# Folding the stage between the layers into the second layer's pipeline

## What is computed

```python
x_prev = jnp.concatenate([jnp.zeros((B, 1, D)), x[:, :-1]], axis=1)
write_lines = exterior(x_prev @ w1w.T, x @ w2w.T)      # per head, 6 components, unit length
read_lines = exterior(x @ r1w.T, x @ r2w.T)
Jw = einsum('bthi,ij->bhtj', write_lines, _J6)
outer = Jw[..., :, None] * Jw[..., None, :]            # 6 x 6, symmetric
M_all = decayed cumulative sum of outer over t, shifted by one token
rd_M = einsum('bhti,bhtij->bhtj', rd, M_all)
score_M, score_M2 = sum(rd_M * rd), sum(rd_M * rd_M)
mem_score = (1 - alpha) * score_M + alpha * score_M2
gated = mean over heads of sigmoid(mem_score * mem_scale) * sigmoid(x @ memg_w.T + memg_b)
out = (seq_out + gated * (x @ memv_w.T + memv_b)) @ out_w.T + out_b
```

## Time and profile before

| | us |
|---|---|
| median of 3 runs | 2576.94 |
| the three | 2562.86, 2576.94, 2578.11 |
| profiled execution, device time | 2571.01 |
| its span | 2569.2 |
| mean granted TensorE clock | 0.888 of 2.4 GHz |
| TensorE, VectorE, ScalarE, GpSimd busy | 86%, 52%, 39%, 14% |

### The profile page before, as it was taken

One profiled execution on the slowest core, in us unless ns is written; L12 is line 12 of the kernel. 1 busy time (PEld: TensorE's weight loads), 2 busy tenths in 40 slices (PEclk: granted clock), 3 DMA queues, 4 the chain that ended last, 5 costly groups with the idle time before them and its releaser, 6 DMA issues. The chain is left out here.

```text
span 2569.2 us, 38948 instructions
## 1 busy us (share of the span) xinstructions
PE 2203.8 (86%) x13569; PEld 1547.9 (60%) x13637; DVE 1340.0 (52%) x3927; ACT 995.6 (39%) x3145; POOL 362.7 (14%) x639
## 2 busy tenths in 40 slices
PE   8588888889999987897727789899999999999887
PEld 4266665656777764676514456566666666766654
DVE  7245556464635454321149457565656565666441
ACT  3133535445454534352212245444434344444320
POOL 2044252332504142001000000000000000000000
PEclk9767989888899978997859699999999999999988
DMA  8000000001233111445550000000000000000000
GB/s 305 9 5 1 5 5 10 9 9 32 97 103 106 44 38 51 154 175 194 166 168 0 15 10 5 6 5 10 5 5 10 5 10 5 6 5 5 5 1 9
DMA packets 50763, 116.27 MB, mean 45 GB/s; under 512 B 8192, under 2 KB 30464, under 8 KB 46976
## 3 DMA queue, kind: packets, MB, share of 16 engines
q1 hardware_dynamic: 49024, 109.49, 12.6%
q0 software_dynamic: 1536, 4.20, 0.5%
HBM read 90.20 MB, written 23.46 MB: 44 GB/s over the span
## 5 line engine op out<-in xcount | busy, mean ns | idle before, releaser
L690 ACT ACTIVATE PRS<-PT 128x384 f32<-128x384 f32 (+1 forms) x512 | 266.1, 520 | 653.7 <-PE PT L621 653.5
L755 DVE TENSOR_REDUCE negmax<-SM 128x2 f32<-128x512 f32 x432 | 283.5, 685 | 194.3 <-PE SM L584 96.7
L621 PE MATMUL PT<-const_sb,PRS 128*128 128x128 f32 x1664 | 309.6, 304 | 51.7 <-ACT PRS L690 49.5
L705 ACT ACTIVATE PRS<-SM,negmax 128x128 f32<-128x128 f32 x608 | 248.1, 420 | 184.8 <-DVE negmax L755 184.8
L621 PEld LDWEIGHTS PT<-const_sb,PRS 128*128 128x128 f32 x1664 | 206.1, 153 | 147.6 <-issue 97.6
L2758 DVE TENSOR_SCALAR arena<-arena 128x256 bf16<-128x256 bf16 x1024 | 210.3, 279 | 9.9 <-PE SC L2776 9.0
L574 PE MATMUL SM<-haloU,QM 32*128 32x128 f32 (+1 forms) x1056 | 172.9, 376 | 7.1 <-ACT PRS L705 4.7
L574 PEld LDWEIGHTS SM<-haloU,QM 32*128 32x128 f32 x1056 | 131.2, 216 | 22.8 <-ACT PRS L705 8.6
L2776 PE MATMUL SC<-arena,identb 128*128 128x256 bf16 x1024 | 138.2, 278 | 2.4 <-DVE arena L2758 2.4
L636 PE MATMUL OA<-PRS,big 128*32 128x256 f32 (+1 forms) x1024 | 133.7, 387 | 3.0 <-ACT PRS L690 3.0
L574 PE MATMUL SC<-haloU,QM 32*128 32x128 f32 (+1 forms) x480 | 111.3, 388 | 28.3 <-ACT PRS L705 28.3
(11 more groups left out here) (565 smaller groups left out, 4072.3 us busy)
## 6 DMA issues: line engine op xcount, KB each, us to landing
...
arena<-lay SPq DMA_DIRECT2D x1, 7700.5 KB, 21.4
...
arena<-lay SPq DMA_DIRECT2D x1, 3862.0 KB, 20.6
...
```

What stands on the lines that cost most here:

```text
L621: ins = pe.transpose(bank[:, o:o + P], PR[n % 4][:, t, k * P:(k + 1) * P], ident)
L690: act.activation(dst, src, ACT.Copy).then_inc(S("probs_moved"), 1)
L705: ins = act.activation(dst, src, ACT.Exp, bias=negmax[:, h, r:r + 1], accum_out=rsum[:, t, h:h + 1])
L755: st.post(dve.tensor_reduce(negmax[:, ORDER[s], :], two(banks[s % NB]), AX.X, ALU.max, negate=True), S("max_ready"))
```

## The change

The stage between the layers and the `clear_block` behind it go. Two new threads of layer 1 do its work. `memory` (30 pieces) has the gate: VectorE's exteriors; squares on ScalarE instead of VectorE; per row i only the components j >= i of the symmetric matrix (21 scans instead of 36), from which two tiles of products are made (`ROW_A`: the row, `ROW_B`: its mirror in the columns), summed by TensorE in SC, PJ0 and PJ1. `fold` (31 pieces) has the same products, in another order, through the one bank "a". The loads of `feat`, `gate_d` and of the weights stand at the head of layer 1's SyncE program, the weights in three parts, in this order: the first 2560 columns (`lay1_a`), the last 2310 (`lay1_b`, biases and small tables), the 10531 between (`lay1_c`). The piece "turn x" of start(1) writes to a second tile (`XNs`), GpSimd clears `VS_count` once the gate is done, and the feed-forward part takes the products under exchanged names (`fW{1 - br}`, `fV{1 - br}`).

```diff
-        SMs = [SM[0], SM[1], SC]
-        with nc.Block() as block:
...
-                for i in range(6):
-                    fold_pe(pe, 0 if i == 0 else 16 + 3 * (i - 1), 16 + 3 * i)
-                    pe.wait_ge(S("row_ready"), i + 1)
...
-        clear_block()
-
...
+        def fold_pe(pe, ba):
+
+            for u, (pe_part, _) in enumerate(folds):
+                if u == 0:
+                    pe.wait_ge(S("lay1_a"), 16)
+                    pe.wait_ge(S("lay1_b"), 16)
+                if u == FOLDS_FIRST:
+                    pe.wait_ge(S("lay1_c"), 16)
+                ba.fill(pe_part(pe, ba.claim(pe)), "act")
+                yield
+
+        def fold_act(act, sa, ba):
+
+            for u, (_, act_part) in enumerate(folds):
+                bank = ba.take(act, "act")
+                ba.release(sa, act_part(act, bank), "act")
+                sa.settle()
+                yield
...
+        MEMORY_LOOP = [[(0, 6, (0, 3)), (0, 6, (3, 6)), "rows"], [(1, 5, (1, 3)), (1, 5, (3, 6)), "rows"], [(2, 4, (2, 6)), "rows"],
+                       [(3, 3, (3, 6)), "rows"], [(4, 2, (4, 6)), "rows"], [(5, 1, (5, 6)), "rows"]]
+        MEMORY = 10 + sum(len(part) for part in MEMORY_LOOP) + 6
...
+                    if part == "rows":
+                        if i:
+                            dve.wait_ge(S("row_summed"), i)
+                        st.post(dve.tensor_tensor(ROW_A[:, i:6, :], MM[:, i:6, 0:T], bc(RDP[:, i, :], 6 - i), ALU.mult), S("row_ready"))
+                        if i < 5:
+                            st.post(dve.tensor_tensor(ROW_B[:, i:5, :], MM[:, i + 1:6, 0:T], RDP[:, i + 1:6, :], ALU.mult), S("row_ready"))
...
+            act.wait_ge(S("feat_in"), 16 * (B + 1))
...
+            yield from idle(3)
+            pe.wait_ge(S("gated_ready"), 1)
...
-            chains(opened(0))
-            tally(0, (("hot", 0, HOT_FIRST + HOT_REST),))
-            chains((("middle", 0, JOIN),), opened(1))
-            for i in range(1, B):
+            chains((("memory", 0, 4),), (("start", 0, OPEN - 1), ("fold", 0, FOLDS_FIRST)))
+            tally(0, (("memory", 0, MEMORY - 10),), (("fold", 0, FOLDS - FOLDS_FIRST), ("start", 1, 1)))
+            chains((("memory", 0, 6), ("start", 0, 1)), (("start", 1, OPEN - 2),))
+            chains((("start", 1, 1), ("middle", 0, JOIN)), (("hot", 0, HOT_EARLY),))
+            tally(1, (("hot", 0, HOT - HOT_EARLY), ("ask", 0, TURN)))
+            count(0, (("middle", 1, JOIN),), opened(2), (("hot", 1, HOT),))
+            for i in range(2, B):
...
                 sp.dma_start(X1s[0][:], x4_d[1]).then_inc(S("x_in0"), 16)
+                for i in range(B):
+                    sp.dma_start(big[i * H:(i + 1) * H, 0:4096].rearrange("h (m n) -> h m n", m=4),
+                                 feat[i + 1].rearrange("m (h c) t -> h m (c t)", h=H)).then_inc(S("feat_in"), 16)
+                sp.dma_start(Z[:, 0, :], gate_d[1:B + 1].rearrange("b h t -> (b h) t")).then_inc(S("feat_in"), 16)
+                sp.dma_start(arena[:, 0:LAY1_A], lay1[:, 0:LAY1_A]).then_inc(S("lay1_a"), 16)
+                sp.dma_start(arena[:, LAY1_B:LAY1_N], lay1[:, LAY1_B:LAY1_N]).then_inc(S("lay1_b"), 16)
+                sp.dma_start(arena[:, LAY1_A:LAY1_B], lay1[:, LAY1_A:LAY1_B]).then_inc(S("lay1_c"), 16)
```

597 lines of the change are left out of this document (324 added, 273 removed).

## The result

| | before | after |
|---|---|---|
| median, us | 2577.5 (4 runs, 2562.9 to 2578.3) | 2617.3 (4 runs, 2608.0 to 2620.6) |
| ratio | | 1.0168, interval 1.0129 to 1.0206 |
| profiled execution, its span | 2571.0, 2569.2 | 2620.6, 2618.8 |
| mean granted TensorE clock | 0.888 | 0.880 |
| TensorE, VectorE, ScalarE busy, us | 2204, 1340, 996 | 2255, 1321, 1002 |

The changed kernel is 1.7% slower by the ratio, and 40 us by the two medians. I had said 2577, no change, in a range up to 2608. Runs in a slower state of the chip are left out of every ratio and median here: one of e8 (3639.1 us) and two of the kernel before (5008.1 and 2756.4 us). The two profiled executions are 49.6 us apart, 10 more than the medians; what follows accounts for the 49.6, and finds some 6 of them to belong to the one profiled execution and not to the change.

What follows compares the result with a forecast made beforehand. Took TensorE, nearly full, as the bound, with 82 of 311 us idle to win. Stages end at 1458 + 45 + 48 + 64 = 1615 against 1612, + 3 us: 2577 us, no change, range 2553 to 2608.

Steps and rivals of the forecast that it cites:

- no change: Whole kernel: the favoured outcome, 2577 us, its own range 2556 to 2600, chance 0.75.
- Loading: Start of layer 1: features land at 1319.5, first two weight parts at 1325.7, the third by about 1340.
- start(0) and four products: After the weights: 16.9 us for start(0)'s chain and 9.6 for four product steps at 1.2 GHz; tally(0) begins at 1352.2.
- tally(0): Attention with 27 product steps and five row sums woven in: 100 us plus 6 for the clock, ending at 1458.
- The rival of the swinging clock: tally(0): half of TensorE's busy time in slots 1 to 9 at 1.2 GHz, + 31, 2608 us; chance 0.12.
- Gate's end, start(1), middle(0): Between tally(0) and tally(1): gate's tail 13.4, value and memory pieces 15, middle(0) 16.5; together 45 us, where now 18.
- tally(1): Attention with 13 one-hot groups on TensorE, not 8, and late ask pieces: 39.8 + 5 x 1.05 + 3 = 48 us.
- count(0): 16 one-hot groups instead of 8: 56.4 + 7.6 = 64 us, VectorE busy 55 of these, no bound.
- a rival for tally(0) alone: tally(0): interlocks, a row's 3 us wait as in slot 4 in all ten slots, + 27, 2604 us; chance 0.04.
- The clock: TensorE's clock: + 6 us in tally(0), 0.5 until a slot's full stretch lifts it; 0 if high, + 19 if low.
- All behind that is the same list.: After count(0): same list of instructions; forecast called wrong if the stretch from 1612 on changes by over 5 us.

Runs made afterwards that it cites:

- e8: Changed kernel without weaving, products on two banks, the gate's last four pieces and start(0)'s last one beside tally(0): 2562.3 us, ratio 0.9938 to the kernel before.
- e4: Changed kernel without weaving: gate beside start(0) and all products first, through one bank, then tally(0) with one-hot groups: 2580.0 us, ratio 1.0018 to the kernel before.
- e5: Kernel before with all 16 one-hot groups of hot(1) in count(0), four buffers and TensorE using each two steps later: 2584.4 us, ratio 1.0037.
- e9: Changed kernel with four buffers for hot(1) and TensorE taking each group two steps later: 2599.7 us, ratio 1.0114 to the kernel before.
- e1: Kernel before with one added line: in each feed TensorE waits for VectorE's copy of XF: 2580.1 us, ratio 1.0020.
- e11: e8 with hot(0) moved into the time of the loads and the small weights loaded ahead of the features: 2553.0 us, ratio 0.9922 to the kernel before.
- e15: e11 with 14 filling matmuls ahead of the wait for the gate's first row: 2541.3 us, ratio 0.9895 to the kernel before.
- e6: Changed kernel with 26 of the gate's 30 pieces, its end among them, in tally(0): 2620.3 us, ratio 1.0188 to the kernel before.
- e10: Changed kernel with start(1)'s first three pieces ahead of the gate's last matmul on TensorE: 2609.8 us, ratio 1.0163 to the kernel before.
- e13: Changed kernel with 34 unused matmuls on TensorE ahead of its wait for the first weights: 2607.8 us, ratio 1.0143 to the kernel before.
- e7: e4 with its products alternating between two banks in place of one: 2566.7 us, ratio 0.9968 to the kernel before.
- e12: e11 with the features ahead of the weights in the queue, 12 pieces of hot(0) ahead of start(0): 2559.5 us, ratio 0.9936 to the kernel before.
- e2: Kernel before with all 16 one-hot groups of hot(1) in count(0) in place of 8, tally(1) keeping ask(0) alone: 2595.5 us, ratio 1.0082.

## Why the prediction was wrong, point by point

- **Loading.** Right. Features 1321.6 (1319.5 said), weights 1327.5 (1325.7). Timeline of ScalarE and VectorE, first work on each:

```profile
1321.57 0.20 ACT L2555 ACTIVATE small<-const_sb 128x1 f32<-128x1 f32 x1 [32.18 <-DMA Z<-gate_d]
...
1327.44 0.23 DVE L3125 TENSOR_TENSOR gate_s<-parq,arena 128x2 f32<-128x2 f32 x2 [28.19 <-DMA arena<-lay]
```

- **start(0) and four products.** 28.1 us for 26.5, clock 0.50 as said. First scores 1355.6 for 1352.2.
- **tally(0).** Right in the main: 110.4 us for 106, busy 81% for 80, VectorE 56% for 65. The product steps of a slot in TensorE's timeline:

```profile
1394.43 1.98 PE L2334 MATMUL PT<-AM,OUT 128*128 128x512 f32 x4 [0.69 <-ACT arena L2338]
1397.17 1.98 PE L2334 MATMUL PT<-AM,OUT 128*128 128x512 f32 x4 [0.75 <-ACT arena L2338]
```

and a stretch of such slots:

```profile
1373.00:1404.00 31.00, 23.72 (x109) 11.18 (x108) 20.06 (x27) 14.11 (x40) 0.00 (x0) 0.99 0.00 1
```

The steps are 2.74 us apart, 2.7 said. The wait for VectorE's first row was 2.8 us, 3.0 said.
- **The rival of the swinging clock** did not happen in tally(0): 0.99 in this stretch with TensorE busy 77% in cycles through one bank, and 1.00 in e4's. The one fall in these slots lasted 3 us, from 1404.7. The Trainium skill, "TensorE: Matmul & The Clock Gate", section "A second HAM failure mode: psum-queue depth-cycling", tells of such a swing in another kernel, of bf16 matmuls with 512 columns; read as a rule for this one it would have the clock swing, and the trace does not agree. The time it gave, 2608, is near the measured one for another reason.
- **Gate's end, start(1), middle(0).** 51 us for 45. I had the value pieces at 0.5 for half; all three were at 0.5, and so was what lay behind them until 1510.
- **tally(1)** 50.5 for 48.
- **count(0). This is the step that failed:** "count(0) gets 16 instead of 8: + 8.4 ... 56.4 + 7.6 = 64", with "VectorE would be busy ... 55 of these 64: no bound". It took 81.5. VectorE was busy 53.5: nearly as said (my 55 counts nine groups where eight were added, and eight give 53.5). A busy share says nothing of order. Two groups to a slot leave no slot between their making and their use, and TensorE waited 9.4 us for them and lost 12.4 to the clock. I had found just this kind of wait in slot 4 of tally(0), and had priced it as a rival for tally(0) alone. With the longer lag of e5 and e9 the same 16 groups take 69.2 and 68.2 us, 4 to 5 above the 64: the price of the groups was nearly right, and the wait between maker and user was missing.
- **The clock.** The sum counted idle time, took the clock as low where a row showed it low, and added 6 us by guess in tally(0). The idle time came out near the forecast: 86.5 us, where 313.5 us (1301.5 to 1615) less 229 of busy time leave 84.5. What the plan lost are 30 us of low clock, 17 of them between tally(0) and tally(1) and 12 in count(0).
- **"All behind that is the same list."** Nearly, but its time was not: 12.5 us more in these two executions. From count(0) to count(1) after takes 122.4 us where before takes 117.7. Six traces (before, e1, e4, e8, e11, e15) have 117.5 to 117.9 there, with 4.6 or 4.7 lost to the clock; after, e6, e10 and e13 have 122.2 to 122.4 with 7.1 to 7.4, and e7 and e12, whose list is that of e4, 122.0 with 9.6 and 9.5. So it goes with the clock; why it fell was not tested. To count(6) after gains 1.3 back. Behind count(6) 9.1 came on top: 2.8 are the wait that e1 isolates, which I had not seen in the diff, and some 6 belong to the one profiled execution.

In sum: 3 said, + 1.8 landing, + 1.6 start(0), + 4.4 tally(0), + 6 gate's end, + 2.5 tally(1), + 17.5 count(0), + 12.5 behind: 49.3 of the 49.6. Some 6 of the last term are not the change's, which is most of the 10 us by which these executions are further apart than the medians. "No change" could have held only if each of these had been near zero; the largest is a mechanism that the range did not contain, and the others have the same sign, most of them with a clock lower than I had set it.

The Trainium skill says, in the same page's "Step-by-step: what each phase is for", that matmuls stay in program order. The rows of e2 agree: ScalarE was done with the last pair of scores at 1560.61, but the next scores began at 1563.97, behind a group that waited 3.00 us for VectorE.
